# The last expert's first half runs through both products ahead of its second half, and three images of the first fold are moved ahead of the expert next to last

## The reference

```python
def _L0_ffn_ref(x, Wr, W1, b1, W2, b2):          # E, F, CAP = 8, 512, 1024
    x_flat = x.reshape(N, Dd)
    probs = softmax(x_flat @ Wr, axis=0)
    vals, idx = top_k(probs.T, CAP)
    selected = x_flat[idx]                        # 8 x 1024 rows of 128
    h = gelu(einsum('ecd,edf->ecf', selected, W1) + b1[:, None, :])
    out_e = einsum('ecf,efd->ecd', h, W2) + b2[:, None, :]
    weighted = vals[..., None] * out_e
    return zeros_like(x_flat).at[idx.reshape(-1)].add(weighted.reshape(-1, Dd))

x = x + conv_block(layer_norm_over_channels(x))
t = to_tokens(x)
t = t + _L0_ffn_ref(layer_norm(t), Wr, W1, b1, W2, b2)
return from_tokens(t)
```

## Time and profile before

| what | value |
|---|---|
| three runs | 489.19, 490.55 (median), 491.89 us |
| the profiled execution | 488.36 us, with a span of 486.6 us |
| PE busy | 358.3 us, 74% of the span |
| DVE busy | 315.9 us, 65% |
| ACT busy | 253.5 us, 52% |
| POOL busy | 159.0 us, 33% |
| chain that ended last, by engine | PE 45%, DVE 18%, ACT 17%, issue 9%, DMA 7% |
| mean DMA rate over the span | 157 GB/s |

### The profile page before, as it was taken

How to read it: one execution, slowest core, us unless ns; L and a number is a source line. 1 busy time by engine, 2 the same in 40 slices (tenths; PEclk the granted TensorE clock), 3 DMA queues, 4 the chain that set the end, 5 groups by cost and what they waited for, 6 DMA issues and landing times.

```text
span 486.6 us, 7851 instructions
## 1 busy us (share of the span) xinstructions
PE 358.3 (74%) x2459; PEld 245.9 (51%) x2459; DVE 315.9 (65%) x1044; ACT 253.5 (52%) x522; POOL 159.0 (33%) x151
## 2 busy tenths in 40 slices
PE   3878999899999975011237978879795987776675
PEld 2435656665566554001124637648474674375564
DVE  3378898899999777888885775664731242245444
ACT  3359898899999873866106345625454402500000
POOL 4000000000000000000177677878887788455000
PEclk9989999999999985555558979989897996795655
DMA  3346577666774646970022313343452676537998
GB/s 107 119 134 189 182 237 258 206 221 219 248 253 156 197 164 192 373 234 0 0 58 53 97 53 99 38 91 50 80 76 55 184 126 127 122 78 169 296 402 322
DMA packets 39120, 76.19 MB, mean 157 GB/s; under 512 B 7056, under 2 KB 19504, under 8 KB 39088
## 3 DMA queue, kind: packets, MB, share of 16 engines
q1 hardware_dynamic: 26976, 60.56, 39.4%
q0 software_dynamic: 9472, 8.72, 11.0%
q10 hardware_dynamic: 2640, 6.51, 3.5%
HBM read 35.03 MB, written 30.39 MB: 134 GB/s over the span
## 4 chain that ended last, share of the span: by engine, by line
PE 45%; DVE 18%; ACT 17%; issue 9%; DMA 7%; SPq 1%; POOL 1%; DVEq 0%; ACTq 0%; POOLq 0%
PE psC L867 11%; PE psC L697 6%; PE psB L855 5%; ACT ln_tok L521 5%; PE psC L855 4%; DMA x_pad<-moe_sum_late 4%; PE psB L731 3%; PE psD L921 2%; DVE x_all L1373 2%; PE psB L719 2%; ACT x_in L581 2%; DVE conv L1013 2%; ACT act L544 2%; PE psA L834 2%; ACT signs L581 2%
## 5 line engine op out<-in xcount | busy, mean ns | idle before, releaser
L421 POOL DMA_INDIRECT picked<-token_rows,slot_idx x32 | 31.5, 984 | 245.0 <-issue 244.7
L697 PE MATMUL psC<-x_pad,tap_diag 64*64 64x392 f32 x384 | 70.2, 513 | 7.8 <-issue 4.1
L697 PE MATMUL psC<-hid,tap_turned 64*64 64x392 f32 x384 | 70.2, 513 | 0.0
L867 PEld LDWEIGHTS psC<-w,hid 128*128 128x128 f32 x480 | 55.3, 195 | 3.5 <-issue 1.8
L867 PE MATMUL psC<-w,hid 128*128 128x128 f32 x480 | 56.2, 279 | 1.1 <-ACT hid L629 0.9
L697 PEld LDWEIGHTS psC<-x_pad,tap_diag 64*64 64x64 f32 x384 | 28.4, 138 | 38.1 <-issue 30.9
L1327 DVE TENSOR_TENSOR y_sum<-psC,b_rows 128x512 f32<-128x512 f32 x15 | 10.4, 692 | 52.2 <-PE psC L867 52.2
L444 POOL DMA_INDIRECT moe_sum_late<-y_rows,slot_idx x24 | 37.5, 1562 | 17.6 <-DVE y_rows L1335 10.6
L855 PE MATMUL psB<-picked_T,w 128*128 128x512 f32 x64 | 38.9, 741 | 5.1 <-ACT picked_T L609 4.0
L521 ACT ACTIVATE ln_tok<-psA,sm 112x128 f32<-112x128 f32 x112 | 40.8, 477 | 0.9 <-DVE sm L1005 0.9
L629 ACT ACTIVATE hid<-psB,b_T 128x512 f32<-128x512 f32 x32 | 21.8, 686 | 35.8 <-PE psB L855 35.8
(11 more groups left out here) (211 smaller groups left out, 796.3 us busy)
## 6 DMA issues: line engine op xcount, KB each, us to landing
token_rows<-rows SPq DMA_DIRECT2D x16, 422.6 KB, 5.0
x_in<-in_x_dram SPq DMA_DIRECT2D x16, 392.0 KB, 3.3
x_res<-in_x_dram SPq DMA_DIRECT2D x16, 392.0 KB, 3.9
moe_sum<-hid SPq DMA_DIRECT2D x16, 392.0 KB, 4.5
x_all<-x SPq DMA_DIRECT2D x16, 392.0 KB, 3.0
moe_sum_late<-hid SPq DMA_DIRECT2D x16, 392.0 KB, 5.4
out_dram<-act ACTq DMA_DIRECT2D x16, 392.0 KB, 6.1
w<-in_L_ffn_W_dram SPq DMA_DIRECT2D x16, 256.0 KB, 3.2
```

Source lines behind the costliest of these rows:

```text
L421: nc.gpsimd.indirect_dma_start(out=picked_in[k][:, b, :], out_offset=None, in_=rows_dram, in_offset=bass.IndirectOffsetOnAxis(ap=slot_idx[ ...
L697: ins = nc.tensor.matmul(psC[col * HC:col * HC + HC, half, 0:HALF].rearrange("c (h w) -> c h w", w=W), weights[of, n, :], lines[of, q, dy: ...
L867: ins = nc.tensor.matmul((psA if first else psC)[:, h, b * C:(b + 1) * C], hid[:, f, lo:lo + 128], w2[:, q, f * C:(f + 1) * C], start=(f = ...
```

## The change

Three things change in the order of the work; the transfers that SP and GpSimd issue, and their order, stay the same.

- The last expert gets a function of its own on TensorE and VectorE, and two halves on ScalarE. Each half now runs turn, first product, second product before the other half begins. Its first second product goes to psA, as the one of expert 0 does.
- The exponential of its gate is made for each half apart, so ScalarE loads the Exp table and the Gelu table once more than before.
- The 16 images of the first fold are spread in another way: images 0 to 2 ahead of expert 6, image 3 between the first and the second product of expert 7's first half, images 4 and 5 after that second product, and images 6 to 15 after the second half's. Before it was 0 to 3, 4 to 6 and 7 to 15.

Some code that did nothing (`keep_running` with a count of zero) is taken out.

```diff
+FOLDED_EARLY, FOLDED_MID, FOLDED_LATE = 3, 4, 6
...
# ScalarE
+            def last_gate_exps(h):
+                e = E - 1
+                act.wait_ge(s_gat[h][e % BUFS], e // BUFS * (8 * SB) + 8 * SB)
+                if h == 0:
+                    act.wait_ge(s_gt, e)
+                act.sem_inc(s_act, 1)
+                nc.scalar.activation(gate_e[:, 4 * h:4 * h + 4],
...
                 elif e == E - 1:
+                    last_gate_exps(0)
+                    load_gelu()
                     gelus(e, 0)
                     take_turned(e, 1)
-                    gate_exps(e)
+                    last_gate_exps(1)
                     load_gelu()
                     gelus(e, 1)
...
# TensorE
+            def last_expert(e, q, use):
+                pe.wait_ge(s_w1[q], use * 16 + 16)
+                turn_picked(e, 0)
+                hidden(e, q, 0, {})
+                for img in range(FOLDED_EARLY, FOLDED_MID):
+                    turn_first(img)
+                pe.wait_ge(s_w2[q], use * 16 + 16)
+                down(e, q, 0)
+                for img in range(FOLDED_MID, FOLDED_LATE):
+                    turn_first(img)
+                turn_picked(e, 1)
+                hidden(e, q, 1, {})
+                down(e, q, 1)
...
-            for e in range(1, E):
-                expert(e, e % 2, e // 2, e + 3 < E, e + 1 < E)
-            for img in range(7, B):
+            for e in range(1, E - 1):
+                if e == E - 2:
+                    for img in range(FOLDED_EARLY):
+                        turn_first(img)
+                expert(e, e % 2, e // 2, e + 3 < E, e + 2 < E)
+            last_expert(E - 1, (E - 1) % 2, (E - 1) // 2)
+            for img in range(FOLDED_LATE, B):
                 turn_first(img)
...
# VectorE, in expert(): the first half of expert 7 is normalized in expert 6
+                if e == E - 2:
+                    norm_picked(e + 1, 0)
...
+            def last_expert(e, q, use):
+                for h in range(2):
+                    if h == 1:
+                        norm_picked(e, 1)
+                    dve.wait_ge(s_ge, e + 1 + h)
...
+                    if h == 0:
+                        for img in range(FOLDED_EARLY, FOLDED_MID):
+                            add_first(img)
+                    bias_out(e, h)
+                    weigh(e, q, use, h)
+                    if h == 0:
+                        for img in range(FOLDED_MID, FOLDED_LATE):
+                            add_first(img)
```

More of the change, by code:

```diff
@@ L700, in conv_taps @@
                 ins.then_inc(s_conv, 1)
-            def keep_running(times):
-                for _ in range(times):
-                    nc.tensor.transpose(psC[:, 0, 0:128], ident[:, :], ident[:, :])
             def step(pair, u):
@@ L743, in step @@
                     turn_weights()
-                    keep_running(WARM_FIRST)
-                if isinstance(img, int) and img == 1:
-                    keep_running(WARM_SECOND)
                 on, img, q, _ = image(pair, u, 4)
@@ L860, in down @@
             def down(e, q, h):
-                first = isinstance(e, int) and e == 0 and h == 0
-                pe.wait_ge(s_gelu, FT if first else e * (2 * FT) + (FT + 3 + h))
+                first = isinstance(e, int) and e in (0, E - 1) and h == 0
+                pe.wait_ge(s_gelu, e * (2 * FT) + FT if first else e * (2 * FT) + (FT + 3 + h))
                 for b in range(4):
@@ L894, in expert @@
                 for h in range(2):
-                    if isinstance(e, int) and e == E - 1 and h == 1:
-                        for img in range(4, 7):
-                            turn_first(img)
-                        turn_picked(e, h)
                     slot_work = ({2: first_ties}, {1: slot_ranks})[h] if ahead else {}
                     hidden(e, q, h, slot_work)
-                late = isinstance(e, int) and e == E - 2
-                if another and not late:
+                if another:
                     for h in range(2):
@@ L907, in expert @@
                 down(e, q, 1)
-                if late:
-                    for img in range(4):
-                        turn_first(img)
-                    turn_picked(e + 1, 0)
+            def last_expert(e, q, use):
[11 more added lines that the diff above has]
+                down(e, q, 1)
             def turn_first(img):
@@ L1325, in bias_out @@
                 dve.wait_ge(s_l2, e * 2 + h + 1)
-                sums = psA if isinstance(e, int) and e == 0 and h == 0 else psC
+                sums = psA if isinstance(e, int) and e in (0, E - 1) and h == 0 else psC
                 nc.vector.tensor_tensor(y_sum[:, 4 * h:4 * h + 4, :], sums[:, h, :].rearrange("s (b d) -> s b d", d=C),
@@ L1330, in weigh @@
             def weigh(e, q, use, h):
-                dve.wait_ge(s_gt, e + 1)
+                dve.wait_ge(s_gt, e + 1 + (h if e == E - 1 else 0))
                 dve.wait_ge(s_yb, e * 2 + h + 1)
@@ L1373, in add_first @@
                     nc.vector.tensor_tensor(kept, psD[:, a, 0:n], kept, ALU.add).then_inc(s_fk, 1)
-            for e in range(1, E):
-                if e == E - 1:
+            def last_expert(e, q, use):
[4 more added lines that the diff above has]
+                    if h == 0:
+                        dve.wait_ge(s_yr, e * 2)
+                    nc.vector.tensor_scalar(gate[:, 4 * h:4 * h + 4], gate_e[:, 4 * h:4 * h + 4], bc[:, 3, ds(e, 1)], None, ALU.mult)\
+                        .then_inc(s_gt, 1)
+                    if h == 0:
[3 more added lines that the diff above has]
+                    weigh(e, q, use, h)
+                    if h == 0:
+                        for img in range(FOLDED_MID, FOLDED_LATE):
+                            add_first(img)
+            for e in range(1, E - 1):
+                if e == E - 2:
                     for q in range(2):
                         dve.wait_ge(s_x1c[q], 16 * B // 2)
-                    for img in range(4):
+                    for img in range(FOLDED_EARLY):
                         add_first(img)
-                    norm_picked(e, 0)
-                    for img in range(4, 7):
-                        add_first(img)
-                    norm_picked(e, 1)
                 expert(e, e % 2, e // 2, e + 3 < E)
-            for img in range(7, B):
+            last_expert(E - 1, (E - 1) % 2, (E - 1) // 2)
+            for img in range(FOLDED_LATE, B):
                 add_first(img)
```

3 lines of the change are left out of this document (2 added, 1 removed).

## The result

The changed kernel takes 498.35 us (median of four runs, 496.23 to 500.01) against 489.99 us beside it. The ratio of the two is 1.0145, with a 95% interval of 1.010 to 1.019. By the interval it is slower by 4.9 to 9.3 us (the medians differ by 8.4); forecast were 7.2 us and 497.8 us.

What follows compares the result with a forecast made beforehand. A chain of waits with no full engine bounds expert 7, and the folds set the start of the end. Terms 11.3 + 1.7 - 7.6 + 1.8 = +7.2 us on a 490.55 us median give 497.8 us; 8-in-10 range 494.3 to 501.3.

Steps and rivals of the forecast that it cites:

- The wait for the early folds' rows: Ahead of expert 6, TensorE waits for the three early folds' loads, then folds: expert 6 starts 11.3 us later.
- S: Start of expert 6's first product on TensorE, at 381.35 before; forecast at 392.6.
- Expert 6 at the lower clock: Expert 6's first pair of its first product runs at the lower clock after the wait: 1.7 us more.
- Expert 7: From the end of expert 6's second product to the end of expert 7's: 28.5 us, 7.6 less than before.
- One fold more: Behind expert 7's second product, ten last folds instead of nine: 15.6 us become 17.4, so 1.8 more.
- The scatters: GpSimd's scatters of expert 7: the last lands at 448.6, six microseconds ahead of the last fold's end.
- The sum: All terms for the whole kernel together: +7.2 us, with the end unchanged at 39.2 us.
- Sooner loads: Rival: the early folds' loads land sooner, expert 6 is late by 8.1 us, sum +4.0, 494.6 us; chance 8 in 100.
- The clock that holds: Rival: folds keep TensorE at 2.4 GHz in expert 6, expert 7 and the last folds; -0.7, 489.9 us; 6 in 100.
- The lower clock in both second products: Rival: in expert 7 both second products double in time, +14.5, 505.1 us; chance 4 in 100.
- The scatters at the end: Rival: the folds keep up and scatters set the end at 448.6; sum +1.2, 491.8 us; chance 3 in 100.
- A dearer pair: Rival: ScalarE's new pair of table loads in expert 7 costs 2.6 us more; +9.8, 500.4 us; chance 3 in 100.

Runs made afterwards that it cites:

- early_behind_6: Changed kernel with its three early folds, and their adds on VectorE, moved behind expert 6; 491.24 us against 491.40 for the kernel before.
- loads_earlier: Changed kernel with the first fold's first four loads issued ahead of the wait for expert 5's second product; 493.12 us against 491.40 for the kernel before.
- early_alone: Kernel before with only images 0 to 2 folded ahead of expert 6; 500.28 us against 491.40 for the kernel before.
- kept_running: Changed kernel with 56 extra transposes, adding no result, ahead of the three early folds; 498.66 us against 491.40 for the kernel before.
- gelus_first: Changed kernel with expert 7's gate exponentials behind each half's GELUs and the second half's Gelu load dropped; 497.04 us against 492.23 for the kernel before.
- tail_running: Changed kernel with four extra transposes, adding no result, behind each of the last ten folds; 496.34 us against 492.23 for the kernel before.
- woven_whole: Changed kernel with eight images' folds woven into the second products, none ahead of expert 6, expert 7 in the old order; 485.50 us against 492.01 before.
- woven_tail: Changed kernel with eight images woven into second products, GELUs first, four extra transposes behind each of the last eight folds; 481.17 us against 492.01 before.

## Why the prediction was right

- **The wait for the early folds' rows** was the large term, and it held: 11.3 us forecast for S, 11.3 measured (-0.2 to 11.1 behind A). That the two agree so well is luck. The loads landed 0.3 and 0.4 us sooner than assumed, and the third fold, which the forecast started at the landing of its load, waited for VectorE's add instead, which took the gain back. In the four other kernels with the same order up to S it came 11.0 to 13.4 us behind A, up to 1.7 beyond the upper bound of the forecast (11.9 later than before). Both runs that took the wait away (early_behind_6, loads_earlier) won 6.4 and 8.5 us from A to L, and early_alone shows it by itself.
- **Expert 6 at the lower clock**, 1.7 us: measured 1.7 (14.4 to 16.0). In the changed kernel the idle wait is what it followed: TensorE did nothing from 385 to 390.8, and the granted clock was 0.94 at 388 to 389 and 0.50 from 389 until S. Whether that wait is needed for it is open. kept_running filled it, and expert 6 still began at the lower clock (3.49); loads_earlier had the three folds without a wait for loads, and expert 6 began at the full one (1.90); early_behind_6 had them so too, and the clock fell in the third. The size is partly luck as well. In early_alone, gelus_first and tail_running, where the rows came later, the first pair took 2.99, 2.52 and 2.38 us. From A to T the five kernels are 12.8 to 14.1 us longer than the kernel before, with 13.0 forecast.
- **Expert 7**, 7.6 us saved: measured 8.5 (36.1 to 27.6). The stretch was put 0.9 too long: 0.7 of it up to the first half's second product (6.8 instead of 7.5 from T to 418.63), where the turn and copy at the full clock and the GELUs with their sums ready were each a little shorter, and 0.2 in the second half. The rows of the new pair and gelus_first leave no room for anything behind a table load. The drain that the Trainium skill puts there (ScalarE: Activation LUTs, "What ACT_TABLE_LOAD costs") isn't borne out here; the measurement decides.
- **One fold more**, 1.8 us: 1.9.
- **The scatters** stayed under the folds, as forecast, but by 3.5 us and not by 6. The last was issued 8.0 us behind D, where 8.1 were forecast; the forecast gave it the landing of the kernel before, 3.3 us, and it took 6.0. In the runs they come up sooner than the forecast would have it: they set L in early_alone, tail_running, woven_whole and woven_tail.
- **The sum** from A to L is 6.3 us where 7.2 were forecast. The ratio of the runs, 4.9 to 9.3 us, holds both. The forecast of 497.8 us is near the measured 498.35 in part because the sum was put on the higher of two times for the kernel before (490.55, where all four runs of it give 489.99), and in part because the medians differ by 8.4 us, more than the 6.3 from A to L and the 0.5 in the end explain.
- **The rivals.** Sooner loads: these landed in 5.0 and 7.3 us, where 5.3 and 7.7 were assumed. The clock that holds: it was low or fell in all three stretches that this rival named (the pair at 3.54 us, the pair at 3.78 behind two folds in expert 7, the last folds at 1.54). The lower clock in both second products: they took 3.8 us each, at the full one. The scatters at the end: the wait at L ended with a fold. A dearer pair: 3.0 us from its start to the first GELU, with no gap behind a load.

## What to carry to other kernels

Before work is moved ahead on an engine that runs without a gap, look up when its operands are issued: here the loads stood behind the very product that the folds were to follow, so a fill for idle time became 6 us of idle time. A chain of short steps between two engines (here 0.6 us of TensorE in 1.4 to 1.8) was cheapest woven between the blocks of a long product, piece by piece, at 0.7 us an image, and not set between products. And when one chain is shortened, name the next one and its distance first: here 0.4 us lay between the folds and the scatters in the kernel before, and in four of the nine runs the scatters set L. A landing time read where little else was moving (3.3 us for a scatter) isn't the one to expect beside other loads (6.0 and 7.2).

## What the runs showed of the hardware

- The granted clock fell while TensorE had been busy for 1.38 and 0.96 of 2 us, in folds, and not only when it idled (kept_running, 394 to 398). It doesn't always: behind three folds without a wait for loads it was up in loads_earlier and had fallen in early_behind_6. With four extra transposes behind each fold (0.44 us) it stayed at 2.4 GHz for the 15.4 us from D to L (tail_running). Without them it fell in the third or fourth fold behind D in seven kernels, but in early_alone the same folds ran at 2.4 GHz until the ninth. A fold's pace is 1.38 us at 2.4 GHz and 1.79 at 1.2.
- The same load of 392 KB, issued first of four behind the same weights, landed after 5.0 to 7.3 us in the five kernels that wait for it ahead of S.
- Four loads of 392 KB beside a gather of 512 rows delayed the gathered rows by 3.3 us (13.29 against 9.97 us of waiting).
- The last scatter landed after 3.3 us in the kernel before and after 6.0 in the changed one, where loads of the fold ran beside it. The DMA rate was 71 GB/s around the first (443 to 447.2) and 238 GB/s around the second (447 to 454).
